# Layer 0 of a third period on VectorE, a start-up unit held back, and one row transfer issued by ScalarE

## The chip, the cores and the metric

The kernel runs on one core of a Trainium2 chip. The metric is the device time of one execution in microseconds (us). The kernel before was timed in three runs; a fourth execution was profiled. In the profile PE is TensorE, PEld its weight loads, DVE is VectorE, ACT is ScalarE, POOL is GpSimd and SP is SyncE; a "q" behind a name is the queue (sequencer) of that engine.

## What is computed

A recommendation model: 32 embeddings of width 16 are looked up for each of 1,024 samples, three layers of a compressed interaction network (CIN) are built on them, and a small tower of dense layers turns their sums into one number a sample.

```python
e = jnp.stack([tbl_f[ids[:, f]] for f in range(32)], axis=1)        # 1024 x 32 x 16
x0 = xk = e
for W in (W0, W1, W2):                                              # each 32 x h x 64
    xk = relu(jnp.einsum('bmd,bhd,mhk->bkd', x0, xk, W))            # 1024 x 64 x 16
    outs.append(jnp.sum(xk, axis=2))
h = jnp.concatenate([*outs, dense_ctx], axis=1)                     # 1024 x 208
y = relu(relu(h @ W_top1 + b_top1) @ W_top2 + b_top2) @ W_top3
```

All is float32. In layer 0 both factors are the embeddings, so each pair of fields is needed only once.

## The kernel before, in words

The batch goes in 16 **periods** of 64 samples (1,024 columns of samples times embedding width), and each period in two **streams** of 512 columns (`s` = 2q and 2q+1). Period 0 starts in two halves, so that work can begin before all of its embeddings are there.

For each period GpSimd gathers the embeddings (16 indirect DMAs, `gather`, L470). TensorE turns them (`turn_fields`, L682; `turn_first` for the halves of period 0, L692), ScalarE copies them out of PSUM (`fields_out`, L897; `fields_first`, L905), SyncE writes them as a list into DRAM (`list_fields`, L356; `list_first`, with every second of eight transfers issued by ScalarE), and reads them back spread over 128 partitions: `mates`, and eight tiles of `rows` in two groups of four (`rows_in`, L398; in the first period three groups for each half, tiles 0 and 1, 2 to 4, 5 to 7, `rows_of_half`, L371).

**Layer 0.** A product of a tile of `rows` and `mates` (128 x 1,024) goes to TensorE, which sums it with the weights into `acc0` (`layer0`, L698; `layer0_first`, L719 for the halves). Periods below `EARLY_PERIODS` = 2 have five products made by VectorE (`product0`, L610; `product_first`, L601). In the later ones GpSimd makes four (`product0`, L488), one of them from a further tile `across` with four transfers of its own, and ScalarE squares one more tile (`square_fields`, L1050), which SyncE fetches with two transfers (`fields_in`). `SUM0` says behind which pair of units TensorE sums a period's layer 0, `FIELDS_AT` where it turns a period's fields.

**Layers 1 and 2.** ScalarE spreads a layer's sums into inputs x1 (for layer 1) and x2 (for layer 2), in two forms, a (`half` 0) and b (`half` 1). VectorE multiplies them by the rows: one **unit** is four tiles, 128 x 2,048 products (`outer`, L636), and there are four units for each layer and stream (`half` 0 and 1, `u` 0 and 1), 256 in all. TensorE sums them. VectorE writes units in a ring of five places, and waits for TensorE (`s_used`) before it overwrites one.

The order is written out. `FIRST_UNITS` are sixteen units of the two halves of period 0, summed one by one (`outer_alone`, L782): layer 1 of the first half (index 0 to 3), two of layer 2 (4, 5), layer 1 of the second half (6 to 9), two of layer 2 (10, 11), and layer 2 of the second half (12 to 15). Then come **slots** j = 2 to 31 with eight units each; TensorE sums them in pairs of one unit of each of two streams (`outer`, L757). Slot 2 works on layer 1 of streams 2 and 3, slot 3 on layer 2 of stream 2 and layer 1 of stream 4, and so on. `vector_units(j)` is the order on VectorE: the two streams alternate, but in slot 3 two units of a stream come together. `MADE`, `made` and `taken` turn this order into the values that the semaphores are waited for.

`keep_busy` (L705) has TensorE work on operands that nobody reads. Every engine takes its instructions strictly in the order of its own block, and a waiting one holds back all behind it. On ScalarE the start reads: `first_input` (inputs for the halves), `first_z` (sums for the outputs), `fields_out(1)`, and so on, in the order that the diff shows.

## Time and profile before

| | |
|---|---|
| median of three runs | 640.38 us (640.11 to 641.25) |
| the profiled execution | 638.23 us |
| its span, first to last instruction | 636.4 us |
| busy: PE / DVE / POOL / ACT | 585.1 / 581.5 / 443.0 / 371.1 us |
| share of the span | 92% / 91% / 70% / 58% |
| mean granted TensorE clock | 0.984 of full speed |
| DMA | 105.85 MB, mean 166 GB/s |

The span is what the trace covers; the profiled execution's own time is 1.8 us longer. Busy shares are averages over the whole span: an engine can bound one stretch and wait in the next. PE's busy time has modelled ends. In the rows further down "[4.94 <-ACT x2a L959]" means that the engine had been idle for 4.94 us and that ScalarE's instruction of L959 on x2a ended that.

### The profile page before, as it was taken

To read this page: it belongs to the slowest core of one execution; us is meant where nothing else is said; L and a number is where in the kernel's file an instruction comes from. 1 tells how busy PE (TensorE), PEld (TensorE's weight loads), DVE (VectorE), ACT (ScalarE), POOL (GpSimd) and SP (SyncE) were. 2 spreads that over 40 slices of the span, in tenths; PEclk is the share of its full clock that TensorE was granted. 3 is DMA by queue.
4 is the path that set the end of the run, shared out by engine and by line. 5 is a ranking of instruction groups with operands and counts; after the bars stand their busy time and mean duration, and the time that the engine had idled before them with its cause. 6 is when DMAs were issued, how large, how long until landed. Compare 5 with 4: busy or idle time off the path is not lost.

```text
span 636.4 us, 8226 instructions
## 1 busy us (share of the span) xinstructions
PE 585.1 (92%) x3030; PEld 220.0 (35%) x3030; DVE 581.5 (91%) x347; ACT 371.1 (58%) x641; POOL 443.0 (70%) x416
## 2 busy tenths in 40 slices
PE   0678788699898989999999999999999999999998
PEld 0244532233232323333334323333334323334355
DVE  2279976898999999999999999999999999999995
ACT  1147552846756565747676575747676575737551
POOL 6477788797888878886979688886989592703012
PEclk9769999899999999999999999999999999999999
DMA  6663897938293845749291846748391947500000
GB/s 172 183 187 58 318 230 240 340 68 304 60 260 132 214 194 126 283 73 335 49 304 60 212 196 143 266 95 314 61 320 36 233 170 176 234 1 1 0 1 1
DMA packets 33365, 105.85 MB, mean 166 GB/s; under 512 B 8999, under 2 KB 16173, under 8 KB 29485
## 3 DMA queue, kind: packets, MB, share of 16 engines
q1 hardware_dynamic: 24044, 102.72, 51.2%
q0 software_dynamic: 8192, 2.11, 2.7%
q10 hardware_dynamic: 1088, 0.49, 0.4%
q8 instruction: 24, 0.39, 0.2%
q14 instruction: 17, 0.13, 0.1%
HBM read 89.56 MB, written 15.73 MB: 165 GB/s over the span
## 4 chain that ended last, share of the span: by engine, by line
DVE 47%; PE 30%; issue 13%; POOL 7%; DMA 2%; ACT 0%; DVEq 0%; ACTq 0%; POOLq 0%
DVE prod L636 47%; PE accb L757 10%; PE acca L757 9%; POOL emb L470 7%; PE acc L698 3%; DMA emb<-in_table,idx 2%; PE spread L804 2%; PE accb L782 1%; PE acc L782 1%; PE acc L728 1%; PE spread L799 1%; PE spread L800 0%; DMA idx<-in_ids 0%; ACT x1a L959 0%; PE spread L682 0%
## 5 line engine op out<-in xcount | busy, mean ns | idle before, releaser
L470 POOL DMA_INDIRECT emb<-in_table,idx x256 | 244.8, 956 | 81.6 <-issue 68.9
L757 PE MATMUL acca<-prod,w 128*64 128x512 f32 x960 | 215.0, 594 | 4.1 <-DVE prod L636 3.3
L757 PE MATMUL accb<-prod,w 128*64 128x512 f32 x896 | 203.3, 600 | 15.5 <-DVE prod L636 15.5
L636 DVE TENSOR_TENSOR prod<-rows,x1a 128x2048 f32<-128x2048 f32 x64 | 145.5, 2279 | 11.5 <-ACT x1a L959 5.2
L636 DVE TENSOR_TENSOR prod<-rows,x2a 128x2048 f32<-128x2048 f32 x64 | 145.5, 2278 | 5.6 <-ACT x2a L959 4.9
L636 DVE TENSOR_TENSOR prod<-rows,x1b 128x2048 f32<-128x2048 f32 (+1 forms) x65 | 145.5, 2245 | 2.6 <-PE accb L757 1.9
L636 DVE TENSOR_TENSOR prod<-rows,x2b 128x2048 f32<-128x2048 f32 x64 | 145.5, 2278 | 1.1 <-PE accb L757 1.1
L757 PEld LDWEIGHTS acca<-prod,w 128*64 128x64 f32 x960 | 67.2, 137 | 137.0 <-issue 127.0
L757 PEld LDWEIGHTS accb<-prod,w 128*64 128x64 f32 x896 | 61.9, 137 | 149.5 <-issue 107.2
L488 POOL TENSOR_TENSOR prod<-rows,mates 128x1024 f32<-128x1024 f32 x42 | 99.2, 2380 | 4.9 <-DMA rows<-field_dram 4.7
L959 ACT ACTIVATE x1a<-acc 64x512 f32<-64x512 f32 x58 | 33.1, 570 | 95.1 <-PE acc L698 94.4
L492 POOL TENSOR_TENSOR zin<-zin 128x512 f32<-128x512 f32 (+1 forms) x24 | 30.5, 1270 | 77.6 <-ACT zin L971 77.2
L965 ACT ACTIVATE x1b<-acc 32x512 f32<-32x512 f32 x116 | 65.4, 564 | 4.7 <-DVE prod L636 3.0
L698 PE MATMUL acc<-prod,w 128*64 128x512 f32 x236 | 55.6, 592 | 0.0
L971 ACT ACTIVATE zin<-accb 64x512 f32<-64x512 f32 (+1 forms) x30 | 30.8, 1027 | 24.4 <-PE accb L757 21.3
L965 ACT ACTIVATE x2b<-acca 32x512 f32<-32x512 f32 x60 | 33.8, 563 | 16.4 <-DVE prod L636 15.8
L488 POOL TENSOR_TENSOR prod<-across,mates 128x1024 f32<-128x1024 f32 x14 | 33.3, 2379 | 11.4 <-issue 11.2
L971 ACT ACTIVATE zin<-acca 64x512 f32<-64x512 f32 x30 | 31.6, 1054 | 12.9 <-PE acca L757 12.5
L897 ACT ACTIVATE zb_field<-spread 32x256 f32<-32x256 f32 x60 | 22.4, 374 | 16.9 <-PE spread L682 16.1
L971 ACT ACTIVATE zin<-acc 64x512 f32<-64x512 f32 x30 | 31.7, 1058 | 0.5
L965 ACT ACTIVATE x2b<-accb 32x512 f32<-32x512 f32 x56 | 31.5, 562 | 0.8
L782 PE MATMUL acca<-prod,w 128*64 128x256 f32 x192 | 24.9, 415 | 6.3 <-DVE prod L636 4.7
(105 smaller groups left out, 349.1 us busy)
## 6 DMA issues: line engine op xcount, KB each, us to landing
rows<-field_dram SPq DMA_DIRECT2D x30, 2048.0 KB, 11.3
field_dram<-zb_field SPq DMA_DIRECT2D x30, 256.0 KB, 3.2
mates<-field_dram SPq DMA_DIRECT2D x15, 512.0 KB, 4.6
across<-field_dram SPq DMA_DIRECT2D x56, 128.0 KB
emb<-in_table,idx POOLq DMA_INDIRECT x256, 4.9
field_dram<-zb_field SPq DMA_DIRECT2D x30, 128.0 KB, 4.1
rows<-field_dram SPq DMA_DIRECT2D x4, 768.0 KB, 7.2
field_dram<-zb_field SPq DMA_DIRECT2D x15, 192.0 KB, 4.4
```

The costliest lines, as they stand in the source:

```text
L470: pool.indirect_dma_start(out=emb[q % EMBS][:, j * EMB:(j + 1) * EMB], out_offset=None, in_=table, in_offset=bass.IndirectOffsetOnAxis(ap= ...
L488: nc.gpsimd.tensor_tensor(prod0[:, k, :], other, mates[:, :], ALU.mult).then_inc(s_prod0p, 1)
L492: nc.gpsimd.tensor_tensor(by_d[:, :, 0:DH], by_d[:, :, 0:DH], by_d[:, :, DH:EMB], ALU.add).then_inc(s_eight, 1)
L636: nc.vector.tensor_tensor(prod[:, n % RING, t:t + count, :], of_rows, xs, ALU.mult).then_inc(s_prod, 1)
L698: mm = nc.tensor.matmul(to[c * HID:(c + 1) * HID, :], w, operand[:, c * HALF:(c + 1) * HALF], start=first, stop=last)
L757: mm = nc.tensor.matmul(acc[j % 2][side * HID:(side + 1) * HID, :], (w1 if layer == 1 else w2)[:, step, :], prod[:, (made(layer, s, half, ...
L782: mm = nc.tensor.matmul(sums_alone(layer, s)[c * HID:(c + 1) * HID, 0:PART], (w1 if layer == 1 else w2)[:, step, :], prod[:, n % RING, i, ...
L804: mm = nc.tensor.matmul(tower[:, j * width:(j + 1) * width], t2[:, k, j * P:(j + 1) * P], h1[:, k, 0:width], start=(k == 0), stop=(k == TO ...
L897: last = nc.scalar.activation(by_d[:, d, :, :, :], turned[d * FIELDS:(d + 1) * FIELDS, :, :, :], ACT.Copy)
L959: last = nc.scalar.activation(to[h * HID:(h + 1) * HID, :], src, ACT.Relu)
L965: last = nc.scalar.activation(to[block * FIELDS:(block + 1) * FIELDS, :], src[of:of + FIELDS, :], ACT.Relu)
L971: return nc.scalar.activation(by_d[:, c * count:(c + 1) * count, :], src.rearrange("k (d b) -> k d b", b=BT), ACT.Relu)
```

## The change

What it does, in the order of the diff:

- `EARLY_PERIODS` goes from 2 to 3. Layer 0 of period 2 is made by VectorE in five products, which stand behind the eight units of slot 2; GpSimd's four products of that period, the four transfers for `across`, the two for `squares` and ScalarE's `square_fields(2)` go.
- VectorE alternates the two streams in slot 3, as in the other slots.
- TensorE sums layer 0 of period 2 behind slot 2's last pair, in five tiles. Layer 0 of period 3 is summed one pair earlier in slot 4 than before, as in later slots.
- The last of `FIRST_UNITS` (layer 2, second half, `half` 1, `u` 1) is made by VectorE behind the products of period 1, and summed by TensorE behind their sums.
- `turn_fields(1)` stands one unit earlier on TensorE, and `turn_fields(2)` behind the second tile of `layer0` of period 1.
- `keep_busy`: 8 instead of 6 ahead of the first sums, 1 new ahead of `turn_first(1)`, 3 new behind the first half's sums, 2 new at the end of slot 2.
- ScalarE issues the transfer of the second group (tiles 2 to 4) of the first half's rows, after a wait for the first half's lists, instead of SyncE.
- On ScalarE `fields_out(1)` stands ahead of the b form of the input for layer 1 of the second half; `input1(2, 0)` and `input1(3, 0)` stand ahead of `first_z(2, 1)`.

```diff
     EARLY = len(EARLY_TILES)
-    EARLY_PERIODS = 2
+    EARLY_PERIODS = 3
     RING0 = 4
...
             a, b = b, a
-        if j == FIRST_SLOT + 1:
-            return [(*stream, half, u) for half in range(2) for stream in (a, b) for u in range(UNITS)]
         if j == SUBS - 1:
...
     FIELDS_AT = {(FIRST_SLOT, 2): 3}
-    SUM0 = {(FIRST_SLOT, 3): [(k, 2) for k in (*range(L0 - 1), SQUARES, L0 - 1)]}
+    SUM0 = {(FIRST_SLOT, 3): [(k, 2) for k in range(EARLY)]}
     for q in range(4, PERIODS):
...
     for q in range(3, PERIODS):
-        late = q == 3
-        SUM0[2 * q - 2, late] = [(k, q) for k in range(3)]
-        SUM0[2 * q - 2, 1 + late] = [(SQUARES, q), (L0 - 1, q)]
+        SUM0[2 * q - 2, 0] = [(k, q) for k in range(3)]
+        SUM0[2 * q - 2, 1] = [(SQUARES, q), (L0 - 1, q)]
...
     def on_vector(q):
-        return q < 2
+        return q < EARLY_PERIODS
...
+        def rows_of_half(queue, h, g):
+            t, count = FIRST[g]
+            part = bass.AP(field_dram.tensor, (h * LENGTH + t) * HALF, [[HALF, P], [1, count * HALF]])
+            queue.dma_start(rows_first[:, h, t:t + count, :], part).then_inc(s_first[h][g], 16)
+
         def list_eights(queue, h, odd):
...
                 sp.dma_start(mates[:, h * HALF:(h + 1) * HALF], part).then_inc(s_mates, 16)
-
-            def rows_of_half(h, g):
-                t, count = FIRST[g]
-                part = bass.AP(field_dram.tensor, (h * LENGTH + t) * HALF, [[HALF, P], [1, count * HALF]])
-                sp.dma_start(rows_first[:, h, t:t + count, :], part).then_inc(s_first[h][g], 16)
...
                 for g in range(len(FIRST)):
-                    rows_of_half(h, g)
+                    if (h, g) != (0, 1):
+                        rows_of_half(sp, h, g)
             for q in range(1, PERIODS):
...
-            sp.wait_ge(s_prod0p, (PERIODS - 2) * L0)
+            sp.wait_ge(s_prod0p, (PERIODS - EARLY_PERIODS) * L0)
             sp.dma_start(w3_row, bass.AP(w_top3.tensor, w_top3.offset, [[0, P], [1, TOP2]])).then_inc(s_wide, 16)
...
             halve12(0)
-            for k in range(L0):
-                product0(2, k)
             gather_early(4)
...
             halve12(LAST - 1)
-            pool.wait_ge(s_prod0p, (PERIODS - 2) * L0)
+            pool.wait_ge(s_prod0p, (PERIODS - EARLY_PERIODS) * L0)
             nc.gpsimd.memset(ones, 1.0).then_inc(s_ones, 1)
...
                 product_first(0, k)
-            for i, unit in enumerate(FIRST_UNITS):
+            for i, unit in enumerate(FIRST_UNITS[:-1]):
                 outer(*unit)
...
                 product0(1, k)
+            outer(*FIRST_UNITS[-1])
             for j in range(FIRST_SLOT, SUBS):
...
                     outer(*unit)
+                if j == FIRST_SLOT:
+                    for k in range(EARLY):
+                        product0(2, k)
             last_sum3(LAST)
...
             pe.wait_ge(s_w12, 32)
-            keep_busy(acc[1][:, :], 6)
+            keep_busy(acc[1][:, :], 8)
             pe.wait_ge(s_w0sum, 3)
...
                 if k == 1:
+                    keep_busy(acc[1][:, :], 1)
                     turn_first(1)
-            for i, unit in enumerate(FIRST_UNITS):
+            keep_busy(acc[1][:, :], 3)
+            for i, unit in enumerate(FIRST_UNITS[:-1]):
                 outer_alone(*unit)
...
                         layer0_first(k, 1)
-                if i == 3 * UNITS - 1:
+                if i == 3 * UNITS - 2:
                     turn_fields(1, 0)
-                if i == len(FIRST_UNITS) - 2:
-                    turn_fields(2, 0)
             for k in order0(1):
                 layer0(k, 1)
+                if k == 1:
+                    turn_fields(2, 0)
+            outer_alone(*FIRST_UNITS[-1])
...
                         layer0(k, q)
+                    if (j, i) == (FIRST_SLOT, 2 * UNITS - 1):
+                        keep_busy(acc[1][:, :], 2)
             last_tower(len(TOWER) - 1, turned)
...
                 list_eights(act, h, 1)
+                if h == 0:
+                    act.wait_ge(s_listed_first[0], len(EIGHTS) * 16)
+                    rows_of_half(act, 0, 1)
...
             first_z(1, 0)
+            fields_out(1)
             first_input(1, 1, 1)
-            fields_out(1)
             first_z(0, 1)
...
             fields_out(2)
-            first_z(2, 1)
             input1(2, 0)
             input1(3, 0)
+            first_z(2, 1)
             input1(2, 1)
...
             input2(2, 0)
-            square_fields(2)
             input1(4, 0)
```

## Rows read from the trace of the kernel before

**Rows 1.** The page, parts 1 (busy us) and 5 (busy, mean ns, idle before)
```profile
PE 585.1 (92%) x3030; PEld 220.0 (35%) x3030; DVE 581.5 (91%) x347; ACT 371.1 (58%) x641; POOL 443.0 (70%) x416
...
L470 POOL DMA_INDIRECT emb<-in_table,idx x256 | 244.8, 956 | 81.6 <-issue 68.9
```

**Rows 2.** Windows: busy us and count of PE, PEld, DVE, ACT, POOL; clock, DMA
```profile
84.40:107.00 22.60, 19.59 (x96) 6.64 (x96) 17.67 (x8) 10.39 (x18) 18.78 (x16) 1.00 0.84 267
107.00:127.10 20.10, 13.96 (x58) 4.20 (x56) 17.76 (x8) 15.02 (x24) 14.50 (x16) 0.92 0.92 296
127.10:150.00 22.90, 22.50 (x118) 7.44 (x116) 20.51 (x11) 9.37 (x17) 20.24 (x17) 1.00 0.43 100
150.00:330.00 180.00, 172.95 (x854) 57.73 (x852) 180.00 (x83) 118.29 (x194) 147.28 (x135) 1.00 0.62 190
```

**Rows 3.** Timeline of DVE, start-up: start, us, line, out<-in, idle before
```profile
29.25 1.89 DVE L601 TENSOR_TENSOR prod<-rows,mates 128x512 f32<-128x512 f32 x3 [2.13 <-DMA rows<-field_dram]
34.64 4.48 DVE L636 TENSOR_TENSOR prod<-rows,x1a 128x2048 f32<-128x2048 f32 x2 [3.50 <-ACT x1a L913]
...
48.27 4.49 DVE L636 TENSOR_TENSOR prod<-rows,x1a 128x2048 f32<-128x2048 f32 x2 [0.37 <-ACT x1a L913]
```

**Rows 4.** Timeline of DVE from 66 to 150 us
```profile
70.42 4.47 DVE L636 TENSOR_TENSOR prod<-rows,x2b 128x2048 f32<-128x2048 f32 x2
74.82 4.62 DVE L610 TENSOR_TENSOR prod<-rows,mates 128x1024 f32<-128x1024 f32 x4
...
84.46 2.29 DVE L636 TENSOR_TENSOR prod<-rows,x1a 128x2048 f32<-128x2048 f32 x1 [3.44 <-ACT x1a L959]
...
107.07 4.49 DVE L636 TENSOR_TENSOR prod<-rows,x2a 128x2048 f32<-128x2048 f32 x2 [4.94 <-ACT x2a L959]
...
149.46 2.29 DVE L636 TENSOR_TENSOR prod<-rows,x1a 128x2048 f32<-128x2048 f32 x1 [1.79 <-ACT x1a L959]
```

**Rows 5.** Timeline of PE from 0 to 140 us
```profile
29.32 0.66 PE L692 MATMUL spread<-ident,emb 128*32 128x128 f32 x8 [0.68 <-DMA emb<-in_table,idx]
...
31.75 1.07 PE L719 MATMUL acc<-prod,h 128*64 128x256 f32 x4
...
76.27 0.67 PE L682 MATMUL spread<-ident,emb 128*32 128x128 f32 x16 [1.31 <-DMA emb<-in_table,idx]
76.88 1.95 PE L782 MATMUL acca<-prod,w 128*64 128x256 f32 x16
78.66 1.03 PE L698 MATMUL acc<-prod,h 128*64 128x512 f32 x4
...
83.05 4.56 PE L705 MATMUL accb<-w 128*128 128x512 f32 x10
...
102.19 3.65 PE L757 MATMUL acca<-prod,w 128*64 128x512 f32 x16
...
113.82 8.78 PE L757 MATMUL accb<-prod,w 128*64 128x512 f32 x32 [3.69 <-DVE prod L636]
```

**Rows 6.** Timeline of ACT from 0 to 150 us
```profile
33.05 1.46 ACT L913 ACTIVATE x1a<-acc 64x256 f32<-64x256 f32 x4 [1.91 <-PE acc L719]
...
53.90 2.89 ACT L921 ACTIVATE x2b<-acc 32x256 f32<-32x256 f32 x8
56.81 1.53 ACT L897 ACTIVATE zb_field<-spread 32x256 f32<-32x256 f32 x4
```

**Rows 7.** Line L398 from 65 to 66.3 us: issues, and time to landing
```profile
L398 SPq DMA_DIRECT2D rows<-field_dram x2: 432/432/433, 65.5 to 65.9; - x2
...
DMA to landing us min/median/max: 8.7/11.2/13.6
```

**Rows 8.** Timeline of POOL from 0 to 150 us
```profile
77.16 1.97 POOL L470 DMA_INDIRECT emb<-in_table,idx  x1 [0.30 <-issue]
...
126.65 2.38 POOL L488 TENSOR_TENSOR prod<-across,mates 128x1024 f32<-128x1024 f32 x1
```

**Rows 9.** Chain of waits in order of time: start, us, what
```profile
69.58 6.56 DMA emb<-in_table,idx
```

## The prediction

> **What bounds the kernel now.** I read the page first: VectorE is busy for 581.5 of 636.4 us [rows 1]. That share says little by itself, so I cut the span into stretches by the slots of the loop [rows 2]. From 150 to 330 us VectorE is busy for 180.00 of 180 us, with TensorE at 172.95: there the multiplications of L636 set the time, and nothing that this change touches lies there. An edit can therefore only pay ahead of 150 us, and what it pays there should reach the end unchanged. The same table gives the idle time of VectorE ahead of that: 4.9 us in 84.4 to 107.0, 2.3 us in 107.0 to 127.1, 2.4 us in 127.1 to 150. VectorE's timeline [rows 3, 4] names the waits. It starts outer units at 34.64 after 3.50 us for x1a, and again at 48.27. The last of the sixteen start-up units ends at 74.8, the layer-0 products of period 1 end at 81.0 (84.46 less 3.44), and slot 2 starts only at 84.46, because x1a waits for TensorE's layer-0 sums. Slot 3 waits 4.94 us for x2a (107.07), then 2.3 us for TensorE to free ring places, and slot 5's second unit waits 1.79 us for x1a (149.46).
>
> Unit costs, all from those timelines. An outer unit of VectorE comes every 2.2 us (74.82 less 70.42, for two) [rows 4]. A layer-0 product of 1,024 columns comes every 1.1 us (4.62 for four), so five take 5.55. On TensorE a start-up unit takes 1.95, a pair of units 3.65, five layer-0 tiles 4.4 (83.05 less 78.66), a turn 0.67, one keep-busy matmul 0.91 (ten records and 4.56 for five) [rows 5]. A gather of GpSimd takes 1.25 with its issue (244.8 and 68.9 us over 256) [rows 1]. ScalarE needs 1.2 from the last sum to x1a or x2a (102.19 and 3.65, to 107.07) [rows 4, 5].
>
> **Part 1, the start (rows by ScalarE, keep-busy matmuls).** The second group of the first half's rows (768 KB) leaves SyncE and is issued by ScalarE, which waits there for the lists. ScalarE has nothing else then. SyncE's own issue takes 0.43 for each group [rows 7], so the group can start some 0.9 us earlier, and the third group 0.4 earlier. Against it, the group now shares the DMA engines with mates and group 0, whose two products ended at 27.12 before; VectorE then waited 2.13 us for group 1, to 29.25 [rows 3]. At 0.63 a product (1.89 for three) group 0 was there by 25.8. It can land anywhere from there to about 28.3 (all three transfers ending together, at the pace at which they came before), and the five products end between 30.7 and 31.5 against 31.14.
>
> The trace shows group 0 and group 1 one behind the other on one queue, 3.4 us apart (25.8 and 29.2) [rows 3]. The Trainium skill, page "DMA: Bandwidth & Descriptors", section "Issuing engines are not separate DMA queues", says that transfers begun by different engines run on the same 16 DMA engines and interleave, so that only issue time is saved. By that rule group 0 is pushed to 28.3 and group 1 gains under 1 us; it speaks against this edit, and the late chain of the first rival is what it would do here.
>
> The eight keep-busy matmuls (two more) run to about 24.1 instead of 22.3. Before, TensorE then idled until the first product and worked at half its speed (1.2 GHz): the four matmuls of 256 columns at 31.75 took 1.07, as long as four of 512 columns at 78.66 (1.03) [rows 5]. If the clock stays at 2.4 GHz, the last sum (32.8) follows the last product (31.14) by 0.6 instead of 1.7, 1.1 us earlier, and the first four units and the second half's sums, ahead of VectorE's 48.27, may bring another 1.2. Against it stands one keep-busy matmul ahead of turn_first(1): 0.9 us, or 1.7 at half clock. The turn ran 29.32 to 29.98, ScalarE's copies and four DMA issues follow it to 33.05, where x1a starts [rows 5, 6], so a late turn delays x1a one for one. Taken together the unit that started at 48.27 starts between 47.1 and 49.5. I take 47.75 (**-0.5**), nearer to the warm case, since three more keep-busy matmuls lie ahead of the first unit.
>
> **Part 2, fields_out(1) ahead of x2b.** The turn of period 1 moves one unit up and ScalarE copies its fields before first_input(1,1,1). VectorE's queue wants x2b 8.8 us after its 48.27, and ScalarE had it ready 0.4 us ahead (53.90 + 2.89) [rows 3, 6]. With 1.53 us of copies in front, x2b is late by 1.1 to 1.2 even if the fields are turned in time; up to 1 us more if period 1's gathers land late, of which I have no row. I take **+1.4**. In exchange the fields are out at about 55.2, not 58.34. SyncE issued the rows 7.1 and 7.6 us after the fields were out, and they took 8.7 and 13.6 us [rows 6, 7], so they landed at 74.2 and 79.6; now at 71.1 and 76.5.
>
> **Part 3, the unit held back.** The fifteenth unit now ends at 72.6 + 0.9 = 73.5, and product0(1) follows it at once, its rows being there (74.2 would have been too late before). VectorE does 5.55 of products and the 2.2 of the held unit, to 81.3. TensorE: the fifteenth unit 1.95, turn_fields(2) 0.67, five tiles 4.4, and x1a 1.2 make 8.2 to 8.3 us after 73.5. So slot 2 starts at 81.8, where before it took 11.84 us from 72.62 to 84.46: -3.6, and with part 1 and part 2 **-2.7** so far. The turn now stands among the sums; it waited for gathers until 76.27 before [rows 5] and is reached at about 77.2, so it should not wait. The held unit's sums and five keep-busy matmuls keep TensorE until 87.8, 1.6 after the first pair is ready, and it catches up with 3.65 against 4.4 a pair.
>
> **Part 4, layer 0 of period 2 on VectorE.** Removed: four products of GpSimd (2.38 each, 9.5 us) [rows 8], six transfers for across and squares (0.64 MB, and at 0.43 an issue 2.6 us of SyncE ahead of the rows) [rows 7], and one Square. Added: five products, 5.55 us, on the engine that bounds. They stand after slot 2's eight units, 81.8 + 17.6 = 99.4, just where VectorE waited 4.94 for x2a. TensorE ends slot 2 at 103.05 and x2a is there at 104.2, hidden. The fifth product needs the first tile's sum (104.0), costing 0.2, so VectorE is free at 105.1. Cost against before: 5.75 less 4.94, **+0.8**; slot 3 starts at 105.1 (107.07 before). Their rows: fields_out(2) ends at about 79.5, and with the 7.1 and 7.6, 8.7 and 13.6 of period 1 [rows 7] they land at 95.3 and 100.7, 4 and 3 us ahead of need. If that cover fails, each us is paid in full.
>
> **Part 5, slots 3 and 4.** Slot 3 now alternates the streams, so its second unit needs x1a of stream 4: TensorE's 103.05, five tiles 4.4, x1a 1.2, that is 108.65, where VectorE is ready at 107.3: a wait of 1.35. Before, TensorE idled 3.69 us ahead of slot 3 and ran its first 32 matmuls in 8.78 where two pairs take 7.3, the granted clock being 0.92 over that stretch [rows 2, 5]; VectorE paid 2.3 us for ring places. Now two keep-busy matmuls fill most of that gap and a pair is complete every 4.4 us, so I put the ring waits at nothing: 1.35 less 2.3, **-0.95**. In slot 4 the sums of period 3 are asked for one pair earlier. Slot 4 starts at 124.05, its first pair is summed at 132.1. GpSimd goes on with its held gathers when slot 3's first pair is used (114.5), takes 7.5 for six gathers and 7.1 for three products, and is done at 129.1 (126.65 was their start before [rows 8]), 3 us ahead. The last sum is then at 140.15 and x1a at 141.35, where the second unit of slot 5 is due at 143.85. The 2.4 us idle of that stretch go: **-2.4**.
>
> GpSimd's gathers beside VectorE's products are slowed a little (one beside those of 74.82 took 1.97, where the mean is 0.96) [rows 1, 4, 8]; the 9.5 us that it is spared are more than that. The Trainium skill, page "SBUF — State Buffer", section "Who interferes with whom", gives a reason: a VectorE instruction with two SBUF inputs contends with GpSimd instructions that read SBUF; by that rule five more such products could hold GpSimd by at most their 5.55 us, under the work it is spared.
>
> **Sum.** -2.7 + 0.8 - 0.95 - 2.4 = -5.25 us at 150 us, and the same at the end. The profiled execution took 638.23 (its span of 636.4 and 1.8 around it), so it would become 633.0. The median of the runs shown is 640.38, 2.15 above it; the forecast for the median is **635.1**.
>
> **Rivals.** (1) *The late start.* Group 0 lands at 28.3 and the clock is at half when the keep-busy matmul and the turn come: the turn ends at 32.7, x1a starts 2.6 later, 1.2 of it is still there at 49.5, x2b adds 1.4, and slot 2 starts 1.0 us earlier than before, not 2.7. Total -3.5: 636.8. For it: the shared DMA engines; against: every later step stands. (2) *The warm start.* Both groups land well and the clock never falls: -1.2 instead of -0.5, x2b costs 1.1, x1a of stream 4 1.0: -6.6, 633.8. (3) *The waits move.* Slot 2 is not earlier (x2b and the turn eat part 3) and of parts 4 and 5 the products' +0.8 is paid in full but the rest comes at half, because ring waits return: 0.8 - 1.7 = -0.9, 639.5. (4) *Slower.* turn_fields(2) now stands between the second and third sum, and TensorE takes nothing past it. Each us that period 2's last gather lands after 77.2 delays x1a and so the whole of VectorE. In the trace it landed at 76.1, 6.56 after its issue, beside period 1's rows [rows 9]. From 79.9 on the first 2.7 are gone; from 83.7 on (5.25 + 1.3 later) the kernel is slower; at 85 it is 643. Against it: those rows now end at 76.5, so the gather has a free way after that. That the change doesn't do what it says I leave out: the idle 4.94 us lie just where the products go.
>
> **How the numbers follow.** Forecast 0.58 (own range 634 to 636.3), late start 0.17, warm start 0.11, waits move 0.08, slower 0.06. Measured differences under 0.2% (1.3 us) can't be told from none. Faster by more: 0.85 (forecast, both starts, less 0.01), same 0.09, slower 0.06. The range leaves out the slower case, the waits that move and the far edge of the warm case: 632.4 to 638.4.
>
> **What would show it.** In the changed profile: slot 2's first unit near 81.8; five L610 products at 99.4 with no DMA named before them; slot 3 from 105.1 with a wait of about 1.4 for x1a before its second unit and no ring waits; x1a in slot 5 with no wait; slot 5 some 5.2 us earlier; x2b waited for at 56 to 58. Wrong would be: a DMA as the releaser of the products, a turn L682 that waits before 80, GpSimd's products named before L698 in slot 4, or new VectorE waits beyond 150 us.

## The result, and the profile after

| | before | changed |
|---|---|---|
| first comparison: median of four runs | 640.25 us (639.46 to 641.25) | 636.0 us (634.84 to 636.31) |
| ratio, 95% interval | | 0.9929 (0.9911 to 0.9947) |
| measured again beside the experiments b1 to b3: 29 and 12 runs | 638.58 us (636.33 to 641.28) | 635.38 us (633.7 to 636.44) |
| ratio, 95% interval | | 0.9941 (0.9923 to 0.9959) |
| the profiled execution, and its span | 638.23, 636.4 us | 636.31, 634.5 us |

The change is 0.6% to 0.7% faster: 4.25 us between the medians, where 5.25 were forecast. The two profiled executions differ by only 1.9 us. The kernel before spreads over 5 us from run to run on one chip (636.33 to 641.28, with granted clocks of 0.981 to 0.989), and its profiled execution of 638.23 is shorter than all four runs of the first comparison.

First the page of the changed kernel, part 1, then the stretches of [rows 2]. The 5.4 us of products are there (581.5 to 586.9 busy), and VectorE is idle for 0.8, 1.4 and 0 us where it was idle for 4.9, 2.3 and 2.4 [rows 2]. The stretch from 150 us on is as full as it was.

```profile
PE 589.5 (93%) x3046; PEld 221.8 (35%) x3046; DVE 586.9 (92%) x352; ACT 370.6 (58%) x640; POOL 436.8 (69%) x412
```

```profile
84.40:107.00 22.60, 21.68 (x110) 7.96 (x112) 21.82 (x13) 11.57 (x21) 17.93 (x20) 1.00 0.81 266
107.00:127.10 20.10, 16.85 (x72) 5.00 (x68) 18.72 (x10) 14.38 (x23) 11.89 (x13) 1.00 0.94 300
127.10:150.00 22.90, 22.02 (x118) 7.50 (x118) 22.90 (x12) 14.21 (x25) 20.03 (x18) 1.00 0.57 145
150.00:330.00 180.00, 173.43 (x856) 57.67 (x852) 180.00 (x83) 116.19 (x189) 148.25 (x137) 1.00 0.62 189
```

VectorE's timeline (start, us, line, operation, what ended the idle time before it), against [rows 3, 4]. First one line of the kernel before, the wait ahead of the last product of the second half, then the changed kernel:

```profile
47.20 0.69 DVE L601 TENSOR_TENSOR prod<-rows,mates 128x512 f32<-128x512 f32 x1 [1.28 <-PE acc L719]
```

```profile
28.29 3.10 DVE L597 TENSOR_TENSOR prod<-rows,mates 128x512 f32<-128x512 f32 x5 [21.34 <-DMA rows<-field_dram]
38.37 4.48 DVE L632 TENSOR_TENSOR prod<-rows,x1a 128x2048 f32<-128x2048 f32 x2 [6.98 <-ACT x1a L921]
...
51.07 4.49 DVE L632 TENSOR_TENSOR prod<-rows,x1a 128x2048 f32<-128x2048 f32 x2 [0.37 <-ACT x1a L921]
...
61.22 4.49 DVE L632 TENSOR_TENSOR prod<-rows,x2b 128x2048 f32<-128x2048 f32 x2 [1.10 <-ACT x2b L929]
...
76.61 5.76 DVE L606 TENSOR_TENSOR prod<-rows,mates 128x1024 f32<-128x1024 f32 x5
...
85.34 2.29 DVE L632 TENSOR_TENSOR prod<-rows,x1a 128x2048 f32<-128x2048 f32 x1 [0.78 <-issue]
...
102.94 5.99 DVE L606 TENSOR_TENSOR prod<-rows,mates 128x1024 f32<-128x1024 f32 x5
...
112.36 2.29 DVE L632 TENSOR_TENSOR prod<-rows,x1a 128x2048 f32<-128x2048 f32 x1 [1.24 <-issue]
```

The first outer unit starts at 38.37, not 34.64; the unit of 48.27 at 51.07; slot 2 at 85.34, not 84.46; slot 3 at 108.84, not 107.07. The first unit is 3.7 us later and the fifth only 2.8: the wait of 1.28 us ahead of it has shrunk to 0.27. The five products of period 2 (102.94) show no wait and hide the one for x2a. Slot 3 has one wait, 1.24, and slots 4 and 5 none: their units come every 2.2 us.

TensorE and ScalarE, against [rows 5, 6]. First TensorE's first tile in the kernel before:

```profile
26.66 1.12 PE L719 MATMUL acc<-prod,h 128*64 128x256 f32 x4 [4.37 <-DVE prod L601]
```

```profile
29.13 1.12 PE L719 MATMUL acc<-prod,h 128*64 128x256 f32 x4 [5.34 <-DVE prod L597]
...
31.04 2.08 PE L705 MATMUL accb<-w 128*128 128x512 f32 x2
33.04 0.66 PE L692 MATMUL spread<-ident,emb 128*32 128x128 f32 x8
...
80.60 0.68 PE L682 MATMUL spread<-ident,emb 128*32 128x128 f32 x16
...
110.95 1.98 PE L705 MATMUL accb<-w 128*128 128x512 f32 x4
114.70 3.65 PE L757 MATMUL accb<-prod,w 128*64 128x512 f32 x16 [1.77 <-DVE prod L632]
```

```profile
36.78 1.46 ACT L921 ACTIVATE x1a<-acc 64x256 f32<-64x256 f32 x4 [1.91 <-PE acc L719]
...
56.74 1.53 ACT L902 ACTIVATE zb_field<-spread 32x256 f32<-32x256 f32 x4
58.30 2.89 ACT L929 ACTIVATE x2b<-acc 32x256 f32<-32x256 f32 x8
```

TensorE idles 5.34 us ahead of the first tile and then has the halved clock (1.12 for four matmuls), as it had before after 4.37 us. One keep-busy matmul (two records in the trace) takes 2.08 at that clock, the second half's turn ends at 33.70 instead of 29.98, and x1a is begun at 36.78 instead of 33.05. Late in the start `fields_out(1)` (56.74) stands ahead of x2b, and VectorE waits 1.10 for it. `turn_fields(2)` (80.60) does not wait.

**One time table for all.** In every profile of this study, on any chip, the time from the second unit of slot 5 to the end of the span is 487.0 us, within 0.03. Everything that differs lies ahead. These are VectorE's starts of outer units, read from the timelines. "14 to slot 2" is the time from the end of the fifteenth unit (index 14) to the start of slot 2's first; "slot 2 to slot 5's second" is the time between the starts of these two units.

| kernel | first unit | fifth unit | 14 to slot 2 | slot 2 | slot 2 to slot 5's second | to the end | span |
|---|---|---|---|---|---|---|---|
| before | 34.64 | 48.27 | 11.76 | 84.46 | 65.00 | 486.98 | 636.4 |
| changed | 38.37 | 51.07 | 8.66 | 85.34 | 62.19 | 486.98 | 634.5 |
| changed, profiled again (b0) | 36.29 | 48.98 | 8.66 | 83.26 | 62.19 | 486.98 | 632.4 |
| rows by SyncE (b1) | 35.09 | 47.51 | 8.65 | 81.78 | 62.22 | 486.99 | 631.0 |
| x2b first (b2) | 37.32 | 50.02 | 10.79 | 85.25 | 62.19 | 486.98 | 634.4 |
| unit not held (b3) | 37.30 | 49.72 | 10.59 | 85.95 | 62.19 | 486.99 | 635.1 |

From it the two profiled executions compare as: start (to the fifth unit) +2.8, fifth to fifteenth unit +1.2, nearly all of it the wait for x2b, from there to slot 2 -3.1, slot 2 to slot 5 -2.8 (65.00 to 62.19), sum -1.9.

### The profile page after: what moved, and what is told of

Same layout as the page of the kernel before. It is cut to its first block, busy times and chain, and to the rows that moved or that the text cites. A ratio compares the mean times of both kernels' runs of the same rounds, so it can differ in the third digit from the quotient of the medians.

```text
span 634.5 us, 8252 instructions
## 1 busy us (share of the span) xinstructions
PE 589.5 (93%) x3046; PEld 221.8 (35%) x3046; DVE 586.9 (92%) x352; ACT 370.6 (58%) x640; POOL 436.8 (69%) x412
## 3 DMA queue, kind: packets, MB, share of 16 engines
q10 hardware_dynamic: 1232, 1.28, 0.7%
## 4 chain that ended last, share of the span: by engine, by line
DVE 49%; PE 23%; issue 10%; DVEq 0%; ACT 0%
DVE prod L632 49%; PE acca L757 8%; PE accb L757 7%; PE spread L804 2%; PE acc L698 2%; PE accb L782 1%; PE acc L782 1%; PE spread L799 1%; PE spread L800 0%; PE acc L728 0%; PE accb L834 0%; PE spread L682 0%; PE spread L808 0%; PE accb L827 0%; DVE mates L669 0%
## 5 line engine op out<-in xcount | busy, mean ns | idle before, releaser
L468 POOL DMA_INDIRECT emb<-in_table,idx x256 | 247.9, 968 | 88.8 <-issue 68.1
L486 POOL TENSOR_TENSOR prod<-rows,mates 128x1024 f32<-128x1024 f32 x39 | 92.2, 2382 | 4.0 <-DMA rows<-field_dram 3.8
L486 POOL TENSOR_TENSOR prod<-across,mates 128x1024 f32<-128x1024 f32 x13 | 31.0, 2384 | 11.2 <-issue 11.0
L902 ACT ACTIVATE zb_field<-spread 32x256 f32<-32x256 f32 x60 | 22.5, 375 | 16.0 <-PE spread L682 15.2
```

The costliest lines, as they stand in the source:

```text
L468: pool.indirect_dma_start(out=emb[q % EMBS][:, j * EMB:(j + 1) * EMB], out_offset=None, in_=table, in_offset=bass.IndirectOffsetOnAxis(ap= ...
L486: nc.gpsimd.tensor_tensor(prod0[:, k, :], other, mates[:, :], ALU.mult).then_inc(s_prod0p, 1)
L902: last = nc.scalar.activation(by_d[:, d, :, :, :], turned[d * FIELDS:(d + 1) * FIELDS, :, :, :], ACT.Copy)
```

## The experiments

All kernels are the changed one with something undone. The theory: parts 3 to 5 of the prediction hold, and the start costs because ScalarE's transfer makes the first group of rows late, so that the keep-busy matmul and the turn come late. Rivals: the start's delay is taken up later anyway; the gain is the held unit's alone; only the clock decides.

**The chips.** The kernels b0 to b3 ran on a quiet chip. On two other chips (a1 to a5, c1 to c4) every kernel, the one before too, took some 30 us more, with medians of 672.16 and 671.16 for it. There TensorE's matmuls come one or a few at a time from about 45 to 65 us, 0.7 us or multiples of it apart, and again near 100; ahead of TensorE's own instructions the profile names "issue", and no engine or DMA. TensorE's timeline with rows by SyncE (a1):

```profile
40.26 2.76 PE L781 MATMUL acca<-prod,w 128*64 128x256 f32 x17 [0.25 <-DVE prod L631]
44.74 0.38 PE L781 MATMUL acca<-prod,w 128*64 128x256 f32 x1 [1.73 <-issue]
45.47 0.56 PE L781 MATMUL acca<-prod,w 128*64 128x256 f32 x1 [0.34 <-issue]
47.57 0.70 PE L781 MATMUL acca<-prod,w 128*64 128x256 f32 x2 [1.55 <-issue]
```

So on these two chips I read the stretches outside of these places, and of the end only large differences.

**1. Rows by SyncE again** (a1 on a delayed chip, b1 on the quiet one).

```diff
-                    if (h, g) != (0, 1):
-                        rows_of_half(sp, h, g)
+                    rows_of_half(sp, h, g)
...
-                if h == 0:
-                    act.wait_ge(s_listed_first[0], len(EIGHTS) * 16)
-                    rows_of_half(act, 0, 1)
```

> The changed kernel with one part undone: SyncE issues the second group of the first half's rows, as before. Theory A (ScalarE's transfer runs beside mates and the first group and delays the first group): the first VectorE product starts near 25.8 us instead of 28.3, the turn of the second half ends near 31.0 instead of 33.7, the first outer unit starts near 35.6 instead of 38.4, and the gain of 2.8 us reaches the end: about 633.2 us. Rival B (the start's delay is taken up later, by the waits ahead of slots 2 and 3): the first unit is as early, but slot 2 and the end are within 0.5 us of the changed kernel, about 636. Rival C (group 0 is late for another reason, such as the transfers of the start): 28.3 stays.

> The changed kernel with the rows' second group issued by SyncE again. On the last chip its first outer unit started at 33.5 us, where a kernel with the changed start had 37.6. Theory A (ScalarE's transfer delays the first group and with it the turn): 3 to 4 us of that reach the end, 0.5% to 0.6% below the changed kernel of this call. Rival B (taken up later, by the wait for x2b, the gathers or period 1's rows): less than 1 us of it reaches the end.

The changed kernel beside it:

> The changed kernel itself, beside the others of this call, so that they have it on the same chip. Every theory: ratio to the kernel before near 0.993, first outer unit of VectorE near 38.4 us, slot 2 near 85.3, where no further delay of the chip lies between.

Measured on the quiet chip: b1 632.2 us (631.2 to 632.96), ratio 0.9893 (0.9863 to 0.9923); the changed kernel 635.38, ratio 0.9941 (0.9923 to 0.9959). So giving the transfer back is worth 3.2 us at the end, as theory A had it, and b1 beats both kernels: its slowest run is below the fastest of the changed kernel's twelve (633.7). The profiled pair shows less, 631.0 against 632.4, with 1.2 us of it at the first unit (35.09 against 36.29). Part of the 3.2 goes with the clock. Five of b1's six runs have a mean granted clock of 1.0, and one of the changed kernel's twelve; that one took 633.7 where the five have a median of 632.19, so at the same clock the transfer is worth about 1.5 us (one run against five). That answers the rival "only the clock decides" as far as one run can. VectorE and TensorE of b1:

```profile
25.62 1.29 DVE L596 TENSOR_TENSOR prod<-rows,mates 128x512 f32<-128x512 f32 x2 [17.84 <-DMA rows<-field_dram]
28.77 1.90 DVE L596 TENSOR_TENSOR prod<-rows,mates 128x512 f32<-128x512 f32 x3 [1.86 <-DMA rows<-field_dram]
35.09 4.49 DVE L631 TENSOR_TENSOR prod<-rows,x1a 128x2048 f32<-128x2048 f32 x2 [4.42 <-ACT x1a L917]
...
47.51 4.49 DVE L631 TENSOR_TENSOR prod<-rows,x1a 128x2048 f32<-128x2048 f32 x2 [0.37 <-ACT x1a L917]
...
81.78 2.29 DVE L631 TENSOR_TENSOR prod<-rows,x1a 128x2048 f32<-128x2048 f32 x1 [0.78 <-issue]
```

```profile
26.46 0.65 PE L718 MATMUL acc<-prod,h 128*64 128x256 f32 x4 [2.01 <-DVE prod L596]
...
27.55 1.12 PE L704 MATMUL accb<-w 128*128 128x512 f32 x2
29.65 0.46 PE L691 MATMUL spread<-ident,emb 128*32 128x128 f32 x8 [0.97 <-DMA emb<-in_table,idx]
```

Group 0 is multiplied from 25.62 on, group 1 from 28.77; in the changed kernel all five products start at 28.29 and in its repetition at 27.30. TensorE idles 2.01 instead of 5.34, keeps its full clock (the mean granted clock of b1 is 1.0), the keep-busy matmul takes 1.12 and is over when the gathers land (the turn waits 0.97 for them), and the turn ends at 30.11. On the delayed chip the first unit of a1 started at 33.52 (expected 35.6), and the turn ended at 28.80; the end was 663.45, ratio 0.9875 (0.983 to 0.9919).

**What the rows by ScalarE do.** In the changed kernel, the issues of the three groups and the times from issue to landing (least, median, most), ahead of 22.5 us, and of ScalarE's alone:

```profile
L332 SPq DMA_DIRECT2D rows<-field_dram x2: 432/432/433, 21.4 to 21.9; - x2
L332 ACTq DMA_DIRECT2D rows<-field_dram x1: 363/363/363, 21.0 to 21.0; - x1
...
DMA to landing us min/median/max: 5.6/6.8/8.0
```

```profile
DMA to landing us min/median/max: 5.6/5.6/5.6
```

ScalarE's group lands at 26.6 (20.99 and 5.6), and group 0, which VectorE needs first, at 28.2 (21.38 and the middle one, 6.8). Before, SyncE issued group 0 at 21.5 and group 1 at 22.0, and they landed after 4.2 and 7.2 us, at 25.7 and 29.2. The three groups of before:

```profile
DMA to landing us min/median/max: 4.2/7.2/8.6
```

The group that is needed second now lands ahead of the one that is needed first.

**2. No keep-busy matmul ahead of the second turn** (a2, c4: two delayed chips).

```diff
                 if k == 1:
-                    keep_busy(acc[1][:, :], 1)
                     turn_first(1)
```

> The changed kernel without the one keep-busy matmul ahead of turn_first(1). Theory A (it lies on the path turn, ScalarE's copies and four issues, x1a, first outer unit, and costs 2.0 us at the lower clock): the turn starts near 31.0 instead of 33.0, the first outer unit near 36.4 instead of 38.4, the end near 634.0. Rival B (taken up later, or the last product's sum is what x1a waits for): the end within 0.5 us of 636.

> The changed kernel without the keep-busy matmul ahead of turn_first(1), rows still by ScalarE. Theory A (with the first group late the turn is ready at once, so the matmul lies on the path to x1a and costs 0.9 to 2.1 us by the clock): the end 1 to 2 us below the changed kernel, ratio 0.991 to 0.9925. Rival B (x1a waits for the last product's sum, not for the turn): within 0.5 us of the changed kernel.

Measured: 665.1 us (ratio 0.9899, 0.9856 to 0.9942) and 662.81 (0.9886, 0.9834 to 0.9939), under the delays of these chips, which say nothing of 1 to 2 us. The start lies ahead of the delays. On the same chip as a2, a4 (experiment 4) has the changed start with the matmul. TensorE of a2, then of a4:

```profile
29.39 0.46 PE L692 MATMUL spread<-ident,emb 128*32 128x128 f32 x8
```

```profile
30.28 2.08 PE L707 MATMUL accb<-w 128*128 128x512 f32 x2
32.28 0.66 PE L694 MATMUL spread<-ident,emb 128*32 128x128 f32 x8
```

The turn starts at 29.39 without it and at 32.28 with it, and VectorE's first unit at 34.52 against 37.64. On the other chip the first units are at 35.46 (c4) against 37.16 (c1) and 36.45 (c3). So the matmul costs 1.0 to 3.1 us of the start, more where its clock is halved. What of it reaches the end on a quiet chip was not measured.

**3. The start all as before** (a5, c2: delayed chips).

```diff
-            keep_busy(acc[1][:, :], 8)
+            keep_busy(acc[1][:, :], 6)
...
-                    keep_busy(acc[1][:, :], 1)
                     turn_first(1)
-            keep_busy(acc[1][:, :], 3)
```

and the rows by SyncE as in 1.

> The changed kernel with the whole start undone: rows by SyncE, six keep-busy matmuls, none ahead of the second turn, none behind the first half's sums. Theory A (the start as changed only costs): the first outer unit starts at 34.6 and the one for layer 2 of the first half at 48.3 instead of 51.1, end near 633.2 us, no worse than with the rows alone given back. Rival B (the keep-busy matmuls earn something once the first group is early): this kernel is 0.5 to 1.5 us slower than the one with only the rows given back.

> The changed kernel with the whole start undone: rows by SyncE, six keep-busy matmuls ahead, none ahead of the second turn, none behind the first half's sums. Theory A (the keep-busy matmuls earn their place once SyncE issues the rows, by TensorE's clock): 1 to 1.5 us slower than the kernel with only the rows by SyncE (632.2, ratio 0.9893), ratio near 0.991. Rival B (they earn nothing): the same ratio, 0.9893, within 0.001.

Measured: 663.71, ratio 0.9875 (0.9831 to 0.9919), beside 663.45 and the same ratio for a1 on its chip; and 659.73, ratio 0.984 (0.9784 to 0.9897). The end can't tell whether the keep-busy matmuls earn anything, and nor can the first unit. It is at 34.73 in a5 and 33.52 in a1, but at 33.89 in c2 and 35.09 in b1: the pairs have opposite signs. What the keep-busy matmuls may earn shows from the first unit to the fifth, where only the quiet chip can be read: 13.63 us before, 12.42 in b1. Before, the first four units' matmuls took 9.74 us in a row and VectorE then waited 1.28 for TensorE; in b1 each unit's took 1.95 at the full clock and VectorE did not wait. That the three matmuls behind the first half's sums did it was not tested alone.

**The two edits of the start together.** All profiles, by VectorE's first product, the turn of the second half on TensorE, and VectorE's first outer unit. All three lie ahead of the delays of the chips.

| second group by | keep-busy matmul ahead of the turn | first product | turn starts | first unit |
|---|---|---|---|---|
| SyncE | no (before, a5, c2) | 25.06 to 25.82 | 28.52 to 29.37 | 33.89 to 34.73 |
| SyncE | yes (a1, b1) | 25.37 to 25.62 | 28.35 to 29.65 | 33.52 to 35.09 |
| ScalarE | no (a2, c4) | 27.35 to 27.45 | 29.39 to 30.09 | 34.52 to 35.46 |
| ScalarE | yes (changed, b0, b2, b3, a4, c1, c3) | 27.30 to 28.29 | 30.90 to 33.04 | 36.29 to 38.37 |

Only with both is the first unit late beyond the spread. With SyncE's rows TensorE reaches the turn at about the time at which the second half's last gather lands (it still waits 0.97 us for it in b1, and not in a1), so the matmul is hidden there. With ScalarE's rows but no matmul the turn starts within about 1 us of the others. With both the matmul has no wait to hide in, and its 1.7 to 2.1 us are paid.

**4. Layer 0 of period 2 by GpSimd again** (a4, c1: delayed chips).

```diff
-    EARLY_PERIODS = 3
+    EARLY_PERIODS = 2
...
+            for k in range(L0):
+                product0(2, k)
...
-                if j == FIRST_SLOT:
-                    for k in range(EARLY):
-                        product0(2, k)
...
-                    if (j, i) == (FIRST_SLOT, 2 * UNITS - 1):
-                        keep_busy(acc[1][:, :], 2)
```

with the old `SUM0`, the old order of slot 3 and `square_fields(2)`.

> The changed kernel with layer 0 of period 2 by GpSimd as before, the old order of slot 3 and of slot 4's sums, and no keep-busy matmuls behind slot 2; the start, the held unit and ScalarE's order stay as changed. Theory A (parts 4 and 5 give the gain from slot 2 on: 65.0 us from slot 2's first unit to slot 5's second before, 62.2 in the changed kernel): about 638.8 us, with 4.9 us of wait for x2a ahead of slot 3. Rival B (moving the products is neutral, the held unit and the earlier rows of period 1 make the gain): within 0.7 us of 636.

> The changed kernel with layer 0 of period 2 by GpSimd, the old order of slot 3 and of slot 4's sums, no keep-busy matmuls behind slot 2; start, held unit and ScalarE's order stay as changed. On the chip where it ran before, delays of the chip lay over it. Theory A (parts 4 and 5 give 2.8 us from slot 2's first unit to slot 5's second: 65.0 us before, 62.2 changed): slot 2 as in the changed kernel, then 65.0 us, the end 2.8 us above the changed kernel, ratio to the kernel before 0.998 to 0.999. Rival B (nearly all of the gain comes from the held unit): within 0.7 us of the changed kernel.

Measured: ratios 1.008 (1.0025 to 1.0134) and 1.0101 (1.0047 to 1.0155), where all kernels with the move had 0.984 to 0.990 on these chips. The sign is theory A's and the size is far above it. The stretch from slot 2 to slot 5's second unit is 66.9 us in c1, and 62.19 in each of the six others on these chips (a4's profiled execution took 678.36 us, its median 672.47, and it is used for its start alone). The profiles of c1 and c3 differ by 8.4 us, 4.7 in this stretch and 3.7 ahead of slot 2, where the chips' delays lie; what makes up the rest of the 12.5 between their medians is not shown. On the quiet chip this edit was not undone. There the stretch is 62.19 to 62.22 in b0 to b3, whatever they undo in the start, the held unit or ScalarE's order, against 65.00 before, and c1, which has parts 2 and 3 of the change, has the long stretch; so its 2.8 us belong to parts 4 and 5. Which of the three, the products, the order of slot 3 or the place of period 3's sums, gives how much was not separated. The waits of before are back, VectorE of c1:

```profile
135.54 4.49 DVE L637 TENSOR_TENSOR prod<-rows,x2a 128x2048 f32<-128x2048 f32 x2 [5.48 <-ACT x2a L967]
...
149.82 2.29 DVE L637 TENSOR_TENSOR prod<-rows,x2b 128x2048 f32<-128x2048 f32 x1 [3.19 <-remote]
...
178.75 2.29 DVE L637 TENSOR_TENSOR prod<-rows,x1a 128x2048 f32<-128x2048 f32 x1 [1.79 <-ACT x1a L967]
```

**5. No keep-busy matmuls behind slot 2** (c3, delayed chip).

```diff
-                    if (j, i) == (FIRST_SLOT, 2 * UNITS - 1):
-                        keep_busy(acc[1][:, :], 2)
```

> The changed kernel without the two keep-busy matmuls behind slot 2. TensorE is idle then for about 3.7 us ahead of slot 3, as before, where its first 32 matmuls took 8.78 us instead of 7.3. Theory A (as predicted: the clock falls and ring waits of 1 to 2.3 us return in slot 3): 1 to 2.3 us slower than the changed kernel. Rival B (the alternating order of slot 3 does it alone: a pair is complete every 4.4 us, and even at half clock its sum is in before the fifth unit after it is written): the clock may fall, but no ring wait and no more than 0.5 us at the end.

Measured: 663.98 (one of six runs took 1261 us), ratio 0.9891 (0.9827 to 0.9954), beside 0.9886 and 0.984 on the same chip. TensorE at the start of slot 3, first in c1 (old order), then in c3:

```profile
142.29 8.78 PE L759 MATMUL accb<-prod,w 128*64 128x512 f32 x32 [3.69 <-issue]
```

```profile
137.47 3.65 PE L757 MATMUL accb<-prod,w 128*64 128x512 f32 x16 [3.69 <-DVE prod L632]
```

Both idle 3.69 us, as the kernel before did [rows 5]. In c1 and before, the next 32 matmuls take 8.78, and the granted clock falls to 0.50 within them (from 143.2 to 146.0 us in c1, from 114.8 to 116.8 before); in c3 each 16 take 3.65 and the granted clock is 1.00 throughout. And c3's stretch from slot 2 to slot 5 is 62.19, as with the two matmuls. So their absence cost nothing in this execution. Whether the alternating order alone would stand a fallen clock, as rival B has it, stays open: the clock did not fall.

**6. x2b first** (b2, quiet chip).

```diff
-            fields_out(1)
             first_input(1, 1, 1)
+            fields_out(1)
```

> The changed kernel with first_input(1,1,1) ahead of fields_out(1) on ScalarE again. Theory A (the changed order costs its wait of 1.1 us and pays it back by rows that are there in time): the wait for x2b goes, period 1's fields are out 2.9 us later, its first rows land near 77.2 instead of 74.3, where VectorE asks at 75.5; slot 2 starts 0 to 1 us later or earlier, the end within 1 us of the changed kernel. Rival B (the 1.1 us is a plain loss): 1.1 us faster than the changed kernel.

Measured: 636.31 (635.47 to 637.27), ratio 0.996 (0.9942 to 0.9978), 0.9 us above the changed kernel. VectorE of b2:

```profile
58.98 4.48 DVE L632 TENSOR_TENSOR prod<-rows,x2b 128x2048 f32<-128x2048 f32 x2
...
76.41 4.63 DVE L606 TENSOR_TENSOR prod<-rows,mates 128x1024 f32<-128x1024 f32 x4 [1.96 <-issue]
81.54 1.23 DVE L606 TENSOR_TENSOR prod<-rows,mates 128x1024 f32<-128x1024 f32 x1 [0.50 <-DMA rows<-field_dram]
...
85.25 2.29 DVE L632 TENSOR_TENSOR prod<-rows,x1a 128x2048 f32<-128x2048 f32 x1 [0.28 <-issue]
```

The wait for x2b is gone (58.98 follows 54.58), and the units from the fifth to the fifteenth take 1.2 us less; then VectorE waits 1.96 ahead of period 1's products and 0.50 for its second group of rows, and 14 to slot 2 takes 10.79 instead of 8.66. Theory A's trade is there: 2.1 us lost against 1.2 gained is the 0.9 us between the medians. The twelve runs of each kernel overlap (635.47 to 637.27 against 633.7 to 636.44), so the sum of the two stretches is the better evidence that the changed order is the better one.

**7. The unit not held back** (b3, quiet chip).

```diff
-            for i, unit in enumerate(FIRST_UNITS[:-1]):
+            for i, unit in enumerate(FIRST_UNITS):
                 outer(*unit)
...
             for k in range(EARLY):
                 product0(1, k)
-            outer(*FIRST_UNITS[-1])
```

and the same on TensorE.

> The changed kernel with the sixteenth unit made and summed ahead of period 1's products again. Theory A (the held unit covers TensorE's five sums and x1a): the unit's sum of 1.95 us lies ahead of the layer-0 sums, slot 2 starts 1.5 to 2 us later (near 87 instead of 85.3), the end 0.25% above the changed kernel. Rival B (the gain of that stretch comes from the earlier rows and the place of the turn alone): within 0.5 us of the changed kernel.

Measured: 637.47 (636.91 to 638.4), ratio 0.9991 (0.9971 to 1.001): 2.1 us above the changed kernel; in the profiles 1.9 of it, and nothing else behind the start, lies in 14 to slot 2 (10.59, not 8.66). VectorE of b3:

```profile
77.47 5.76 DVE L606 TENSOR_TENSOR prod<-rows,mates 128x1024 f32<-128x1024 f32 x5
85.95 2.29 DVE L632 TENSOR_TENSOR prod<-rows,x1a 128x2048 f32<-128x2048 f32 x1 [2.72 <-issue]
```

The wait ahead of slot 2 is 2.72 us, where the changed kernel has 0.78. The earlier fields (experiment 6) and the held unit (experiment 7) are each worth about 2 us of that stretch, and together 3.1: they overlap.

## Why the prediction was right, and where it was not

- **The start (part 1) is the term that was mis-sized.** I put it at -0.5 (47.75, from 47.1 to 49.5), and it was +2.8 in the profiled execution (51.07, outside these bounds) and +0.7 in the other profile of the same kernel (48.98). Group 0 landing late was in my bounds (28.3, measured 28.2) and so was the halved clock, but I took a value nearer to the warm case, and did not add up the case with both. The rival "late start" had the chain and was itself too mild: turn ended at 32.7 (33.70), x1a 2.6 later (3.7), slot 2 at 83.5 (85.34; 83.26 in b0). Its keep-busy matmul took 2.08 us and not 1.7. The sentence drawn from the Trainium skill, page "DMA: Bandwidth & Descriptors", section "Issuing engines are not separate DMA queues", was borne out: the transfer begun by ScalarE interleaved with SyncE's and moved group 0 from 25.7 to 28.2. Experiment 1 gives the edit back, and its fifth unit at 47.51 (47.75 forecast) and slot 2 at 81.78 (81.8) are where I had put them. In part that is luck, since the forecast was for rows issued by ScalarE. My reason for a gain, that TensorE at its full clock is 1.2 us faster from the first unit to the fifth, is borne out: 13.63 us before, 12.42 in b1.
- **Part 2** was right: 1.10 for 1.4. The fields are out 2.9 us earlier counted from the fifth unit (7.20 us behind it, 10.07 before), and with the late start at the same time as before (58.27, 58.34). Experiment 6 shows that to be worth more than the wait.
- **Part 3** was right: 3.1 us for 3.6. The turn took its place among the sums without a wait. Rival 4 (the late gather) did not occur.
- **Part 4** was right: the products and their wait for the first sum take 5.9 us (102.94 to 108.84) where 5.75 were forecast, x2a is hidden, the rows are in time. The slowing of the gathers beside products is there and small: two of them (at 103.80 and 105.28) take 1.17 and 1.97 us instead of 0.94, 1.3 us in all, under the 9.5 that GpSimd was spared.
- **Part 5** was right in size: a wait of 1.24 for 1.35, no ring waits, and x1a of slot 5 in time; parts 4 and 5 together gave 2.8 us for 2.55. Its cause is only half shown. I credited two keep-busy matmuls with keeping the clock; experiment 5 has the same stretch without them.
- **The sum.** With the start as measured the profiled pair gives -1.9, not -5.25. That the medians differ by 4.25 is partly the step from the profiled execution of before to its median: I added 2.15 us to the forecast for the changed kernel, whose median and profiled execution agree to 0.3. Runs of before spread over 5 us, and one profile of it can't stand for them all. So the forecast of 635.1 against 636.0 is nearer than its steps were, and that is luck: for the profiled execution I had 633.0, and it took 636.31. The error of 3.3 us in the start was for the most part covered by a profile of the kernel before that happened to be 2 us under its median.

## What to carry to other kernels

A transfer moved to another queue to start earlier competes with the ones ahead of it; if they are needed first, it can put them off and cost more than the issue time saved. Here the first group landed 2.5 us later, and a keep-busy matmul behind it lost the wait in which it had been hidden. Small edits to one chain are to be added up together. Put added work of the bounding engine where that engine is already waiting for another one's last result, and move the inputs so that they are there by then. Matmuls that hold a clock up must not stand ahead of the instruction on which the next stage waits.

## What was not expected of the hardware

- On two of three chips TensorE's instructions came 0.7 us or multiples of it apart for some 20 us, with 30 us more in all, in each of these kernels; the profile names only "issue". Its cause is open.
- After an idle time of 3.69 us ahead of the same matmuls the granted clock fell to one half for some us in two kernels (8.78 us for 32 matmuls) and stayed full in a third (3.65 for 16). An idle time of one length does not settle the clock.
- GpSimd's gathers slow down beside one kind of VectorE product and not beside the other. Three gathers of the changed kernel start beside the layer-0 products of period 1 (76.61 to 82.37), whose two inputs, `rows` and `mates`, both lie in SBUF, and take 1.81 to 1.97 us. Beside outer units, whose input x1 or x2 lies in PSUM, they take 0.94 to 0.95. In every profile of this study each gather behind 16 us that took over 1.1 us started beside a layer-0 product. GpSimd of the changed kernel:

```profile
73.08 0.94 POOL L468 DMA_INDIRECT emb<-in_table,idx  x1 [0.30 <-issue]
...
78.95 1.97 POOL L468 DMA_INDIRECT emb<-in_table,idx  x1 [0.31 <-issue]
```
